# A counting loop in bodies of two edge tiles with two slots, in place of four and four

## The reference, cut to what matters

```python
src = randint(20000, 0, 1250)
dst = minimum((1250 * uniform(20000) ** 2.0).astype(int32), 9999)
src, dst = src[argsort(dst)], dst[argsort(dst)]       # edges sorted by dst
x = layernorm(x + attention_4(x, edges))
x = layernorm(x + relations_8(x, edges, edge_type))   # divides by the count of (dst, type)
x = layernorm(x + convolution(x, edges, edge_weight)) # divides by sqrt of summed weights of dst
x = layernorm(x + attention_12(x, edges))
```

## Time and profile before

| | us |
|---|---|
| median of 3 runs | 3701.8 |
| range of the runs | 3701.58 to 3707.79 |
| profiled execution, own time | 3705.44 |
| its span | 3703.8 |
| PE busy in the span | 3248.3 (88%) |
| DVE busy | 2209.0 (60%) |
| ACT busy | 1335.1 (36%) |
| POOL busy | 972.8 (26%) |
| mean granted clock of PE | 0.933 |

### The profile page before, as it was taken

How to read it: one execution, slowest core, us unless ns; L and a number is a source line. 1 busy time by engine, 2 the same in 40 slices (tenths; PEclk the granted TensorE clock), 3 DMA queues, 4 the chain that set the end, 5 groups by cost and what they waited for, 6 DMA issues and landing times. The chain is left out here.

```text
span 3703.8 us, 60518 instructions
## 1 busy us (share of the span) xinstructions
PE 3248.3 (88%) x20691; PEld 3029.7 (82%) x20691; DVE 2209.0 (60%) x4064; ACT 1335.1 (36%) x2521; POOL 972.8 (26%) x1002
## 2 busy tenths in 40 slices
PE   3997885988997859999998989999998897699994
PEld 3886674877886859999997979999988585699994
DVE  4986635655676451113876721128877555999896
ACT  1244222323332111112445511114545221487683
POOL 1100743444445300002555600005546100000000
PEclk9988897999998979999999999999999899899897
DMA  2033333122121123335776643337767301100001
GB/s 75 22 91 114 101 111 100 45 92 78 46 70 31 68 86 110 99 113 183 240 238 212 213 140 99 99 122 242 241 191 225 132 14 47 44 1 1 1 1 42
DMA packets 139185, 386.91 MB, mean 104 GB/s; under 512 B 26804, under 2 KB 68321, under 8 KB 138962
## 3 DMA queue, kind: packets, MB, share of 16 engines
q0 software_dynamic: 56848, 215.18, 18.9%
q1 hardware_dynamic: 82114, 168.89, 13.3%
HBM read 284.69 MB, written 99.32 MB: 104 GB/s over the span
## 5 line engine op out<-in xcount | busy, mean ns | idle before, releaser
L1777 PE MATMUL bank<-w_hi,xT_hi 128*125 128x384 f32 x1920 | 651.8, 339 | 18.8 <-ACT arena L1512 10.3
L1778 PE MATMUL bank<-w_lo,xT_hi 128*125 128x384 f32 x1920 | 650.1, 339 | 0.0
L1779 PE MATMUL bank<-w_hi,xT_lo 128*125 128x384 f32 x1920 | 650.0, 339 | 0.0
L1512 ACT COPY arena<-bank 125x384 f32<-125x384 f32 x320 | 153.9, 481 | 809.0 <-PE bank L1779 713.4
L722 ACT ACTIVATE arena<-arena,low 125x1250 f32<-125x1250 f32 x170 | 228.0, 1341 | 438.5 <-DVE low L734 438.1
L2195 DVE CAST w_hi<-w_raw 128x2304 fp32r<-128x2304 f32 x36 | 49.0, 1361 | 563.1 <-PE bank L1779 514.3
L883 DVE SCALAR_TENSOR_TENSOR row_lo<-arena,edges,row_hi 128x768 fp32r<-128x768 f32 x300 | 304.7, 1016 | 119.9 <-ACT row_hi L852 77.8
L1777 PEld LDWEIGHTS bank<-w_hi,xT_hi 128*125 128x125 f32 x1920 | 357.7, 186 | 20.6 <-issue 13.3
L1778 PEld LDWEIGHTS bank<-w_lo,xT_hi 128*125 128x125 f32 x1920 | 357.6, 186 | 0.1
L1779 PEld LDWEIGHTS bank<-w_hi,xT_lo 128*125 128x125 f32 x1920 | 357.5, 186 | 0.1
L742 PE MATMUL bank<-ident,arena 125*125 125x125 f32 x1700 | 237.0, 290 | 99.0 <-DVE tsc_lo L629 48.3
(11 more groups left out here) (356 smaller groups left out, 6874.5 us busy)
## 6 DMA issues: line engine op xcount, KB each, us to landing
y_early<-arena SPq DMA_DIRECT2D x200, 187.5 KB
w_raw<-in_L_gnn_W_dram POOLq DMA_DIRECT2D x32, 1152.0 KB
arena<-own_mask_d SPq DMA_DIRECT2D x50, 610.4 KB
y_late<-arena SPq DMA_DIRECT2D x120, 187.5 KB
arena<-in_L_gnn_W_dram SPq DMA_DIRECT2D x8, 1536.0 KB
h_d<-arena SPq DMA_DIRECT2D x40, 250.0 KB
arena<-h_d SPq DMA_DIRECT2D x4, 2500.0 KB
wadj_d<-arena SPq DMA_DIRECT2D x10, 625.0 KB
```

What stands on the lines that cost most here:

```text
L1777: pe.matmul(b, xT_hi[:, k, v], w_hi[:, h, k], start=(k == 0), stop=False)
L1778: pe.matmul(b, xT_hi[:, k, v], w_lo[:, h, k], start=False, stop=False)
L1779: ins = pe.matmul(b, xT_lo[:, k, v], w_hi[:, h, k], start=False, stop=(k == KD - 1))
```

## The change

One constant is changed. `U` is both the number of tiles in a body and the number of slots, so the loop, the two buffers, the two lists of semaphores and the table of bodies all follow it.

```diff
     assert TAIL
-    U = 4
+    U = 2
     WIN = 32
     NW = 4 * NT
     CT = 4 * WIN
```

## The result

| | before | after |
|---|---|---|
| median, runs of both side by side | 3706.3 us (7 runs) | 3716.7 us (7 runs) |
| range | 3701.6 to 3711.8 | 3709.6 to 3727.2 |
| span of the profiled run | 3703.8 | 3708.0 |
| mean granted clock of PE | 0.933 | 0.934 |

The ratio is 1.0033, with a 95% interval of 1.0016 to 1.0049. The forecast was 3741 us, with a range of 3722 to 3767: the direction was right and the size was not.

The account below looks back on a forecast made before the run. DVE, the slower per tile, was taken to pace the counting loop, with PE nearly full too. Long windows +16 and short windows +24 made 40 us on 3705.4, giving 3745.4, or 3741 as a median; range 3722 to 3767.

Parts of the forecast that it names:

- The tiles and bodies: Counting loop: 236 tiles in 59 bodies become 220 tiles in 110 bodies, 16 tiles fewer and 51 body ends more.
- the slot's turn: Counting loop: reusing a slot takes 1.93 us, so two slots give 0.97 us a tile against 0.72.
- the plain window: Counting loop: an ordinary window of four tiles takes about 4.6 us in place of 3.90, +0.7.
- The sum of +40: Counting loop: 16 us more in the 12 long windows plus 24 us in the 28 short ones.
- The parts of a group: Four short windows in the counting loop: first +0.2, behind L2011 +2.0 (5.9 us), plain +0.7, last +0.5; 3.4 us a group.
- Body ends at nothing: Counting loop: the 51 added body ends fit into existing gaps and cost nothing; upper bound 29 us.
- rival (d): Counting loop: body ends lie on the path, half the upper bound, +15 us, 3756 us; chance 0.12.
- The clock in the loop: Counting loop: PE's granted clock is 0.90 today; low stretches dampen the loss, but PE may stay low longer.
- rival (c): Counting loop: PE's clock falls, low for half the loop, about 20 us more, 3761 us; chance 0.15.
- (a): Counting loop: two slots are enough, only the saved tiles show, 11.5 us less, 3690 us; chance 0.04.
- (b): Counting loop: with a slot reuse of about 1.6 us gains and losses balance, within 0.2%; chance 0.04.
- I take the loop's change as passed on one to one: Behind the counting loop: nothing hides a delay, so its 40 us reach the kernel's end in full.

Follow-up runs that it names:

- e4: Kernel before, still with bodies of four tiles, but two slots used in turn: 3733.2 us, 1.0101 of before.
- e2: Changed kernel with 16 more DVE instructions (satisfied waits) near its start, in idle time: 3740.6 us, 1.0125 of before.
- e1: Kernel before with 112 more DVE instructions (satisfied waits) near its start, in idle time: 3674.4 us, 0.9933 of before.
- e6: The changed kernel measured again, beside other runs of the kernel before: 3716.8 us, 1.0046 of before.
- e11: Changed kernel with 8 more DVE instructions near its start: 3742.3 us, 1.0151 of before.
- e3: Kernel before with 206 more instructions on PE alone, near its start in idle time: 3695.9 us, 0.9991 of before.
- e10: Kernel before with 50 more DVE instructions near its start and one added DVE reduction per turn of the last loop: 3706.8 us, 1.0026 of before.
- e7: Changed kernel with one more DVE instruction near its start: 3716.4 us, 1.0052 of before.

## Why the prediction was wrong, step by step

- **The tiles and bodies, the slot's turn, the plain window: right.** 220 tiles; 1.93 us for two in a run, to the hundredth; plain windows 4.64 against 4.6. The sum of +40 up to the dense stage came out as +42.7 in the profiled pair. Over five profiles in pairs with two slots and six in fours with four slots the mean start is 391.7 and 346.8, +45. By the same profiles the first 12 windows take 15.5 more (16 forecast for the long ones) and the other 28 take 28.5 more (24 forecast).
- **The parts of a group: right in sum, by luck.** The window behind L2011 took 6.81 where I had 5.9, at a granted clock of 0.75, and the first of a group rose by 0.7 and not by 0.2. The last of a group got shorter by 0.8 where I had it longer by 0.5. In the group shown above these cancel, 3.6 against 3.4.
- **Body ends at nothing: right.** The comparison of e4 and the change says so, and the pairs are not over 2.1 apart: rival (d) is out.
- **The clock in the loop: right.** 0.88 against 0.90; rival (c) needed under 0.8. Rivals (a) and (b) fall with the turn of 1.93.
- **"I take the loop's change as passed on one to one": the step that failed.** It is true of the delay, as before and e2, e1 and e6 show. But the sum had no term for anything behind the loop, which puts it at nothing. I looked for what a delay would meet and not for what else the edit moves: it took 400 DVE instructions out in front of code that is the same in both kernels. That took the stalls out of the last loop: 24.9 us by e1 against before, 23.8 by e6 against e2. What is left, 42 - 25 = 17, is what e6 measured (+17.7).
- **Still open: the first comparison's +10.4,** 7 us under e6's. The two intervals overlap. The kernel after has the same median in both (3716.7 and 3716.8); it is the kernel before that stood at 3706.3 there and at 3699.1 to 3699.6 in the others, where its runs spread from 3672.9 to 3716.7. In the profiled pair 13.4 us came back between the dense stage and the last loop. That stretch lasts 2913 to 2927 us in e1 to e11, whatever their counting loop, and 2934 in the profile of before; so most of the 13.4 belongs to that one execution and not to the change. Its timeline has eight more rows in that stretch, from 493 to 2734, in which DVE idles 2.1 to 4.3 us by "issue", 21 us together. The profiles of e1 to e11 and of the kernel after have at most two such rows (over 1.9 us) there, and e3, with the same DVE program up to there, has one. They may be the cause; how much of them lay on the path was not worked out.

The signs were in the trace of before: DVE rows with 2.4 to 2.6 us of "issue" at each turn of a loop, and instruction packets in the middle of it. I had read the views of the counting loop only.

## What to carry to other kernels

An edit that changes the number of instructions on an engine moves all of that engine's code behind it. For each hot loop on each engine, look at the row behind its branch for an idle time of "issue", and at the DMA view of the loop for instruction packets, before pricing any edit in front of it. To compare two variants fairly, bring the later loops to the same place with a few instructions in idle time. Where a stage is bound by PE with no gaps, as this last loop is, look at PE's granted clock behind a hole in another engine: holes that made PE idle for about 2 us a turn cost 1.7 to 4.9 times that idle time here (e2 and e10).

## What the runs showed of the hardware that I had not expected

- A DVE loop of 290 instructions is fetched anew at every turn from some places and never from others; DVE stands still for 2.0 to 2.7 us at places 102 and 110, and for 4.3 to 4.8 at 127 and 0. Seven instructions more (e11 against e7) cost 26 us of 3716 (0.7%).
- A stall of 2.63 us a turn cost 37.6 us in four turns (e10), five times PE's idle time.
- With the stalls the last loop's time scatters. Four turns took 293.2 to 312.4 us in the four kernels with stalls of 2.0 to 2.7 us, 317.3 and 325.7 in the two with the longer ones, and 279.4 or 279.5 in all seven profiles without the refetch or the added operation. The whole time of the kernel before spread over 44 us in 35 runs (3672.9 to 3716.7), but e1 had only 6 runs (over 12) and e6 12 (over 17), too few to compare the spreads closely.
- Register-computed addresses on PE: ten matmuls in 1.53 us at a granted clock of 0.50, where they took 1.31 at that level with fixed addresses, and the clock stayed at 0.51 through the loop.
